# Sliced attention on one Trainium2 core: softmax row sums taken over eight pairs of key blocks in place of five groups of two to four

## The reference, cut to what matters

```python
q, k, v = ...                        # [4, 8 heads, 2048, 32]; q, k, v of x's layer norm
attn = einsum('bhqd,bhkd->bhqk', q, k) * scale      # scale = 256 ** -0.5
attn = softmax(attn, axis=-1)
attn_out = einsum('bhqk,bhkd->bhqd', attn, v)
# of the queries e*512 .. e*512+511 only the first 256 / 2**e columns of attn_out are used
```

## Time and profile before

| what | value |
|---|---|
| median of 3 runs | 5153.57 us (5153.51 to 5154.35) |
| span of the profiled execution | 5142.3 us |
| median less that span | 11.3 us |
| the phase at2, exponentials to its last store | about 4224 to 5034 us of the span |
| its steady part, every engine in the same cycle | about 4275 to 4915 us |
| length of a unit there | 53.34 us |
| the next phase's first DMA | 5035.9 us |

### The profile page before, as it was taken

One profiled execution on the slowest core, in us unless ns is written; L12 is line 12 of the kernel. 1 busy time (PEld: TensorE's weight loads), 2 busy tenths in 40 slices (PEclk: granted clock), 3 DMA queues, 4 the chain that ended last, 5 costly groups with the idle time before them and its releaser, 6 DMA issues. The chain is left out here.

```text
span 5142.3 us, 90411 instructions
## 1 busy us (share of the span) xinstructions
PE 4714.6 (92%) x34043; PEld 2092.5 (41%) x34043; DVE 4237.0 (82%) x5517; ACT 3449.7 (67%) x6176; POOL 1333.4 (26%) x881
## 2 busy tenths in 40 slices
PE   6999786797999999999999999999998879999993
PEld 3444452364333333333333333333334445555542
DVE  6999650397899999999999999999993877777736
ACT  4787310132688888888888888888886326666663
POOL 2233220164000000000000000000001229999992
PEclk9999897898899999999999999999998669999996
DMA  5110479688333333343333344333322941222305
GB/s 182 52 53 33 155 247 385 251 280 232 45 53 48 48 48 48 54 54 51 48 48 48 50 54 53 50 48 48 49 34 76 313 128 42 71 70 67 78 10 167
DMA packets 390773, 498.42 MB, mean 97 GB/s; under 512 B 165440, under 2 KB 278880, under 8 KB 373312
## 3 DMA queue, kind: packets, MB, share of 16 engines
q1 hardware_dynamic: 372448, 465.90, 38.7%
q10 hardware_dynamic: 17888, 26.74, 1.5%
HBM read 325.15 MB, written 165.02 MB: 95 GB/s over the span
## 5 line engine op out<-in xcount | busy, mean ns | idle before, releaser
L792 DVE TENSOR_REDUCE at_NM<-at_MX 128x1 f32<-128x1024 f32 (+1 forms) x3008 | 3085.0, 1050 | 299.5 <-PE at_MX L614 270.9
L734 ACT ACTIVATE at_PB<-at_S 128x512 f32<-128x512 f32 x5056 | 2719.4, 597 | 585.9 <-PE at_S L643 466.0
L614 PE MATMUL at_MX<-at_KT,at_QT 48*128 48x512 f32 (+1 forms) x5056 | 1919.7, 455 | 60.2 <-DMA at_VS<-v 45.6
L643 PE MATMUL at_S<-at_QT,at_KT 50*128 50x512 f32 (+1 forms) x5056 | 1899.9, 441 | 6.0 <-ACT at_PB L734 5.8
L655 PE MATMUL at_AV<-at_PB,at_VS 128*32 128x256 f32 (+1 forms) x18304 | 1567.7, 414 | 16.7 <-ACT at_AVS L742 15.7
L643 PEld LDWEIGHTS at_S<-at_QT,at_KT 50*128 50x128 f32 (+1 forms) x5056 | 801.8, 187 | 876.6 <-ACT at_PB L734 772.0
L614 PEld LDWEIGHTS at_MX<-at_KT,at_QT 48*128 48x128 f32 (+1 forms) x5056 | 791.6, 190 | 311.0 <-DVE at_NM L792 217.7
L655 PEld LDWEIGHTS at_AV<-at_PB,at_VS 128*32 128x32 f32 x18304 | 364.6, 108 | 858.6 <-ACT at_PB L734 745.4
L548 POOL CAST at_NMR<-at_NMF 16x128 fp32r<-16x128 f32 x79 | 22.1, 280 | 1625.3 <-ACT at_NMF L747 1625.3
L575 POOL TENSOR_TENSOR at_SUM<-at_SUM,at_PB 128x2048 f32<-128x2048 f32 x90 | 415.4, 4615 | 10.9
L932 PE MATMUL wkv_PQ<-wkv_XT,wkv_WT 128*128 128x512 f32 x768 | 339.6, 600 | 42.5 <-DVE wkv_DL L1052 25.9
(11 more groups left out here) (209 smaller groups left out, 3531.4 us busy)
## 6 DMA issues: line engine op xcount, KB each, us to landing
moe_W<-in_w SPq DMA_DIRECT2D x64, 1024.0 KB, 11.9
at_QT<-qk SPq DMA_DIRECT2D x402, 128.0 KB, 5.2
at_KT<-qk SPq DMA_DIRECT2D x384, 128.0 KB, 6.6
qk<-r_HI SPq DMA_DIRECT2D x52, 512.0 KB, 5.0
qk<-r_LO SPq DMA_DIRECT2D x52, 512.0 KB, 5.3
at_VS<-v SPq DMA_DIRECT2D x96, 256.0 KB, 9.2
at_KT<-qk SPq DMA_DIRECT2D x96, 256.0 KB, 6.2
ycat<-wkv_Y SPq DMA_DIRECT2D x32, 512.0 KB, 2.6
```

What stands on the lines that cost most here:

```text
L614: ins = nc.tensor.matmul(MX[r][:, a, :], q_of(s)[h:h + NQ, b * P:(b + 1) * P], k_of(it, s, b * P // W)[h:h + NQ, (c + a) * W:(c + a + 1) * W],
L643: nc.tensor.matmul(SP_[item(it, s, "score", t)[1]][:, :], k_of(it, s, c)[h:h + NQ + 2, kb * P:(kb + 1) * P], q_of(s)[h:h + NQ + 2, c * W:( ...
L734: nc.scalar.activation(PB[:, t % NPB, :], SP_[r][:, :], ACT.Exp, scale=scale).then_inc(exp_done, 1)
L792: nc.vector.tensor_reduce(NM4[:, b, c:c + 1], MX[r][:, :, :].rearrange("p a n -> p (a n)"), AX_X, ALU.max, negate=True).then_inc(ring_got, 1)
```

## The change

The table of groups alone is changed; all else follows from it.

```diff
-    GROUPS = () if TWO else ((0, 4), (4, 8), (8, 10), (10, 14), (14, 16))
+    GROUPS = () if TWO else tuple((kb, kb + 2) for kb in range(0, NBLK, 2))
     NADD = NBLK - len(GROUPS)
```

## The result

The changed kernel takes 5179.43 us (median of 4 runs, 5178.63 to 5182.86) where the kernel before takes 5153.54 us beside it (4 runs, 5146.32 to 5154.35). The ratio is 1.0056, 95% interval 1.0042 to 1.0070: slower, by 22 to 36 us. Predicted were 5185.2 us, range 5179 to 5192; the span is 5176.8 us where 5173.9 were predicted.

The account below looks back on a forecast made before the run. PE was taken to bound the steady part, POOL mattering only at the ends; 38.7 us of added sums less 7.1 us of waits gave +31.6 us on 5153.6, 5185.2 us (+0.61%), range 5179 to 5192.

Parts of the forecast that it names:

- rival D: Last two units: six additional sums fall into PE's waits for ACT; 5180.0 us, chance 0.06.
- What bounds: Steady part: PE's items alone make the 53.3 us unit; POOL, 97% busy, leaves PE no wait.
- The price of a sums, 0.86 us: PE, three more sums a unit, 45 in all at 0.86 us each, nothing hiding them: 38.7 us added.
- The waits at the ends, -7.1 us: PE's waits for POOL late in unit 13's turn, in the last unit and tail go: 0.42 + 2.07 + 4.6 us.
- The moved wait: Sums at step 22 wait for `norm_done` eight steps sooner, slack 0.5 us; costed at nothing, at most 5.6 us.
- rival C: Normalise too late for the sums at step 22, PE waits in 14 units; 5190.8 us, chance 0.10.
- the sign that the prediction named for rival C: In the profile after, POOL or DVE appears as releaser of a `sums` in every unit.
- rival B: POOL paces ACT's exponentials through old-block additions, 14.6 us of waits real; 5131.9 us, faster, chance 0.04.
- Row against rule: PE's weight loads fill 50%; the skill's rule calls half of PE free, the rows price each sums at 0.86 us.
- rival A: PE has room, added sums pass in its gaps, only 7.1 us count; 5146.5 us, chance 0.05.
- The 11.3 us outside the span: Whole program: the median's 11.3 us over the profiled span, kept in the forecast, 5142.3 to 5153.6 us.
- The distance of the sums: On PE, in the profile after, sums stand 6.98 us apart throughout.

Follow-up runs that it names:

- e1: Changed kernel with the sums at steps 22, 38 and 62 left out (output not the reference's); unit 53.40 us, phase 813.1 us, ratio 0.9987.
- e2: Changed kernel with the additions at steps 8, 24 and 48 done twice, eleven a unit again; unit 55.99 us, phase 856.2 us, ratio 1.0077.
- e3: Kernel before with four groups of four, twelve additions and four sums a unit; unit 57.2 us, phase 882.1 us, ratio 1.0123.
- e4: Kernel before with key blocks 4 to 7 split in two: six groups, ten additions, six sums; unit 54.20 us, phase 828.4 us, ratio 1.0020.
- e6: Kernel before with pairs in the last unit alone, five groups in the other units; unit 53.35 us, phase 816.8 us, ratio 0.9999.
- e5: Changed kernel with the first sums of a unit at step 26 instead of 22; unit 56.00 us, phase 852.3 us, one run, no ratio.
- e8: Changed kernel with SUM and ONES in bf16; unit 50.83 us, phase 775.3 us, ratio 0.9921.
- e9: Kernel before (five groups) with SUM and ONES in bf16; unit 50.12 us, phase 771.4 us, ratio 0.9906.

## Why the prediction was right, point by point

The span's 34.5 us, by the stretches of the two traces. The phase's parts are split at the start of the first values (4228.81 and 4229.73) and at the end of the last exponential (5018.41 and 5055.93), and end with the start of the last normalise:

| stretch | before | after | change | predicted |
|---|---|---|---|---|
| up to the first cast | 4210.6 | 4211.5 | +0.8 | 0 |
| first cast to first values | 18.2 | 18.3 | +0.1 | 0 |
| first values to last exponential | 789.6 | 826.2 | +36.6 | 38.7 - 2.5 = +36.2 |
| last exponential to last normalise | 12.7 | 7.2 | -5.5 | -4.6 |
| behind it | 111.2 | 113.6 | +2.5 | 0 |

The first and the last row can't be put down to the change: over the twelve traces the phase's first cast moves by 13.8 us, and the stretch behind the phase takes from 111.1 to 113.6 us, with the same code in both.

- **The time.** 5179.43 us lies within the range by 0.4 us, and it lies nearer to rival D's 5180.0 than to the forecast's 5185.2. That the number came out inside is in part luck: the runs of the kernel before alone are 17 us apart. What bears the forecast out is the phase, +31.2 us against +31.6, and the unit, 55.97 us against 55.9.
- **What bounds.** PE sets the pace, and POOL's 97% does not. e1 took 27% of POOL's additions away and left units at 53.40 us; e2 put them back under the changed kernel and left them at 55.99. Shown from both sides. POOL was nearer to the bound than the prediction had it: its 51.2 us a unit, with 0.7 for the cast and split, leave out the 0.14 us by which an addition starts later when it needs the one ahead, and the count from e3 is 52.5 of 53.34 us.
- **The price of a sums, 0.86 us.** Measured three ways: (55.97 - 53.34) / 3 = 0.88 for the change, 0.86 from e4, (55.97 - 53.40) / 3 = 0.86 between e1 and the changed kernel. In the last unit too, a block with sums took 5006.01 - 5002.45 = 3.56 us, against 2.70 without, so rival D is out:

```profile
5002.45 1.06 PE L655 MATMUL at_AV<-at_PB,at_VS 128*32 128x512 f32 x8
5003.34 1.04 PE L666 MATMUL at_L<-at_SUM,at_ONES 128*32 128x512 f32 x8
...
5006.01 1.06 PE L655 MATMUL at_AV<-at_PB,at_VS 128*32 128x512 f32 x8
```

- **The waits at the ends, -7.1 us.** e1 shows 7.5 us, 0.9 of them from last sums that ran 1.06 us instead of 1.94. In the changed kernel the tail gave 5.5 instead of 4.6, as its last sums ran 1.07 us and not 1.94. I had left that as it was; in e6 it stayed at 1.94, so the 0.9 us are not sure to come (the granted clock, below).
- **The moved wait.** Right to cost it at nothing: the sums of step 22 are not held up, and moving them off the wait (e5) gave nothing. But the sign that the prediction named for rival C, DVE as releaser of a sums in every unit, did appear (12 times between 4240 and 4960 us, on a weight load), so the sign was a poor one: that releaser alone doesn't show a cost.
- **POOL as releaser of ACT (rival B).** I read the 14.6 us as coincidences. In the steady part they vanished in the changed kernel, and in e1, with no gain in the unit.
- **Row against rule.** The weight loads' share, 50% before, fell to 49% (315.6 of 640 us) as PE got more to do. By the rule of the Trainium skill (Perfetto Trace Analysis, Identifying the Most-Contended Engine) that is room; in this kernel the added sums did not pass in it, each cost its 0.86 us (the change, e4), and rival A is out. The section names the utilisation in FLOPs (MFU) beside that share; the prediction left it out, and it was not worked out here. What told the load of PE was the distance between the starts of its items.
- **The 11.3 us outside the span.** This step was wrong. In the changed kernel's profiled run 5178.63 us stand against a span of 5176.8, 1.8 us outside; in all runs on record that have both figures it is 1.7 to 3.0 us. The execution profiled before was thus some 9 us faster than its median, a difference of runs that the sum carried along. That accounts for most of what separates 5185.2 from 5179.4: of 19 runs of before in one job the median is 5149.68, and 5149.7 + 31.6 = 5181.3 us.
- **The distance of the sums.** Not "6.98 us apart throughout": it is 6.97 to 7.01 us where both stand behind their values, but once a unit 6.1 and once 7.9, where one of the two stands ahead of them (starts at 4389.73, 4395.85, 4402.85 and 4410.72 in the changed kernel's trace). The sum over a unit is the same.

## What to carry to other kernels

When a change moves work between two busy engines, don't compare their busy shares; find the one whose items, added up by the distance of their starts, make the length of the cycle, and price the change at that engine alone. The other engine's relief is worth what it made others wait at the ends of the phase, where the first engine's load is lighter. A table that balances two engines can stand at the crossing, where a step in either direction loses (e3, e4). A cheaper item gives more than a better balance did here: in bf16 both tables beat the kernel before, while their order stayed as it was, five groups ahead by 0.7 us a unit.

## What the runs showed of the hardware

- Eight fp32 matmul instructions of 128x32 against 128x512, in four strips of 32 columns, take 0.86 to 0.89 us from start to start of what follows; the same sums in bf16 are four instructions and 0.24 us (e8 against e9).
- GpSimd's addition over [128 x 2048] takes 4.70 us from two fp32 operands of one buffer and 4.62 with SUM as one of them; into a bf16 SUM it is 4.59 and, with SUM as one operand, 4.12 (e9); one that needs the result of the addition ahead starts 0.14 us after that one's end (4.81 us after its start, where it takes 4.67, e3).
- The last sums of the phase took 1.06 or 1.07 us in the traces of the changed kernel, e1 and e5, and 1.93 or 1.94 in those of before, e2, e3, e4 and e6. It is PE's granted clock: 1.00 (2.4 GHz) in the stretch ahead of it in the changed kernel, 0.50 (1.2 GHz) in e6, where PE had done much the same in the 5 us before, 1.9 us of work against 2.2. The windows of the changed kernel and of e6:

```profile
5056.00:5061.00 5.00, 2.19 (x20) 0.56 (x24) 0.00 (x0) 0.60 (x1) 4.65 (x1) 1.00 0.00 0
```

```profile
5021.00:5026.00 5.00, 1.92 (x16) 0.42 (x16) 0.00 (x0) 0.86 (x2) 4.66 (x1) 0.98 0.00 0
5026.00:5029.00 3.00, 1.94 (x8) 0.20 (x8) 0.00 (x0) 0.85 (x2) 0.00 (x0) 0.50 0.00 0
```

So a tail of this length ends now at one level and now at the other, and 0.9 us hang on it; what decides it is open.
